# A graph-transformer layer on one core: the dense branch's attention, residual and normalization made per tile in the projections

## The chip, the cores and the metric

The kernel runs on one core of one Trainium2 chip. The metric is the device time of one execution in microseconds (us); the median of three runs is given. Besides the five engines TensorE (PE), VectorE (DVE), ScalarE (ACT), GpSimd (POOL) and SyncE (SP), the core has 16 DMA engines. A change of 0.3% can't be told from none.

## The reference, cut to what matters

6250 nodes of 256 numbers, 100000 edges sorted by target, four edge types, four heads of 64. `_layernorm` has no gain; all is float32.

```python
xn = layernorm(x)
# edge branch
xe = xn + segment_sum(edge_emb[type], src) / max(count, 1)
q, k, v = xe@Wq+bq, xe@Wk+bk, xe@Wv+bv
alpha = sum(q[dst]*k[src], per head) / 8
a = exp(alpha - segment_max(alpha, dst))
gnn = segment_sum(a*v[src], dst) / segment_sum(a, dst) + (xe@Ws + bs)
# dense branch: attention over features, so it is one matrix for all nodes
q, k, v = split(xn@w_qkv + b_qkv)
A = softmax(k.T @ v / 8)              # 64x64 for each head
x1 = xn + (q @ A.T)                   # = xn @ w_qf + b_qf
h = layernorm(x1)*norm_g + norm_b
mix = x1 + (gelu(h@w_fc1 + b_fc1) @ w_fc2 + b_fc2)     # 256 -> 768 -> 256
y = x + gnn + mix
out = y + experts(layernorm(y))       # 8 experts of three 256x256 layers, weighted by a softmax
```

## The kernel before

Nodes are worked in 49 tiles of 128 rows (`NW`). The stages follow each other on all engines; each engine's program is written out in order, and semaphores alone couple them. No scheduler decides anything.

**Preparation.** Sorting tables, the histogram of edge types (`r4x`), the normalized `x` in SBUF (`xnode`), also stored to DRAM as `xn_rows`, and the matrix `xn.T @ xn` for the dense attention.

**Projections.** Four tiles make a turn: `turn_types` transposes their type shares, `turn_x` transposes the nodes and adds the edge embeddings in PSUM (L1136, L1140), ACT (`upper`) and DVE (`lower`) split the result into a high and a low part. `project` (L1151) then makes q and skip in one product of 512 columns and k and v in another; each is six matmuls in a reduced float32 form (two halves of the contraction, three pairs of high and low parts). DVE (`evacuate`, L1609 to L1614) adds biases, keeps q in SBUF and adds `x` to skip; SP stores k and v (`kv_rows`) and `x` + skip (`sx_rows`). Between tiles `attend` makes, in eight small steps, the dense branch's matrix `w_qf` and bias `b_qf`.

**Edge pass.** 208 steps of four slots of 128 edges. POOL gathers k and v of the sources into a ring of 12 steps (four gathers a step, L811), after all of `kv_rows` and `sx_rows` is stored. In step i DVE makes one-hots (L1732), multiplies q and k (L1738), sums scores (L1744), weights v of step i-7 (L1791) and adds up the sums of step i-8 (L1805, or L1800 to L1803). PE spreads q to the edges of step i+2 (`spread_q`, L1275) and gathers up step i-7 (`gather_up`, L1286). Every fourth step the segment maxima of 16 slots go from DVE over PE and ACT (Exp) back (L1754 to L1786, L936).

The **dense branch** rides in the same steps: `dense` gives every eight steps a group g of two tiles and a phase p. PE: phase 0 the product with `w_qf` (L1231, full float32), phase 2 transposes, 3 to 5 the first large layer (L1246), 4 to 7 the second (L1253), 7 the next group's transposes (L1220). DVE: phase 0 bias, statistics and variance (L1701 to L1709), phase 1 normalization (L1712, L1714), phases 3 and 4 residual sums (L1718, L1720), phase 7 the last sum (L1726). ACT: Sqrt in phase 0, scaling in phase 2, Gelu in 3 to 5. The result goes to DRAM (`res_rows`).

**Experts.** 13 groups of three or four tiles, eight experts each. `first_part` prepares the next group between the experts of this one: in expert 0's place DVE divides the edge sums, adds `res_rows` (L1878) and takes statistics.

Of the kernel before, what the change touches and what calls it, by code (L numbers as in the profile page):

```python
# [24 lines left out]
def gps_layer_kernel(nc, x, src, dst, etype, edge_emb, Wq, bq, Wk, bk, Wv, bv, Ws, bs,  # L25
# [61 lines left out]
    def done(g):  # L87

        return g + (1 + CREDIT)
# [12 lines left out]
    xnD = nc.dram_tensor("xn_rows", [NW * P, D], F32, kind="Internal").ap()  # L102
# [15 lines left out]
    FC1 = {3: (0, 1), 4: (2, 3), 5: (4, 5)}  # L118
    FC2 = {4: (0,), 5: (1,), 6: (2, 3), 7: (4, 5)}

    with ExitStack() as ctx:
# [21 lines left out]
        m_st = sb("m_st", [P, TG * 6], F32)  # L143
        m_mv = sb("m_mv", [P, TG * 2], F32)
        m_rs = sb("m_rs", [P, TG], F32)
# [34 lines left out]
        emb = pre("emb", [3 * NTYPE, D], F32)  # L180
# [14 lines left out]
        part("gap8", [P, 9 * D + 2 * P + 512], F32)  # L195
        w_glow = part("w_glow", [P, 8 * D], F32R)
        part("gap9", [P, AN + 7400 - 17 * D - 2 * P - 512], F32)
        r4x = part("r4x", [P, 3 * NK], F32R)
        part("gap11", [P, 8 * NSP + NF * QW - 7400 - 3 * NK], F32)
        x_up = part("x_up", [P, 2 * NF * QW], F32R)  # L200
        x_low = part("x_low", [P, 2 * NF * QW], F32R)
        part("gap12", [P, RN + 3008 - 8 * NSP - 5 * NF * QW], F32)
        r4_T = part("r4_T", [3 * NTYPE, 2 * QW], F32R)
        part("gap13", [P, 4500 - 3008 - 2 * QW], F32)
        emb3 = part("emb3", [3 * NTYPE, D], F32R)
        part("gap10", [P, 7112 - 4500 - D], F32)
        w_gup = part("w_gup", [P, 8 * D], F32R)
        parts.close()

# [9 lines left out]
        m_x1 = mid("m_x1", [P, W4], F32)  # L219
# [31 lines left out]
        e_rest = sb("e_rest", [P, 1024], F32)  # L251
        f_res = sb("f_res", [P, WT], F32)
        f_split = sb("f_split", [P, 8 * WT], F32R)
# [3 lines left out]
        e_bol = sb("e_bol", [3 * NE, D + 4], F32)  # L257
        assert 2 * WE == 4 * D + AN and 4 * HG * SL + 2 * WE + 1024 + WT <= RING and 2 * WT <= HELD
# [96 lines left out]
        sxS = [work[:, 1560 + 256 * k:1560 + 256 * (k + 1)] for k in range(4)]  # L355
        zero_g = work[:, 2600:2600 + D + 1]
        r4T = [r4_T[:, QW * b:QW * (b + 1)] for b in range(2)]
        emb_low = work[0:3 * NTYPE, 4200:4200 + D]
        emb_at = [work[0:3 * NTYPE, 4200 + D + i:4200 + D + i + 1] for i in range(2)]
        ATT = {4 * r - 2: r for r in range(1, 9)}  # L360
        ATT_BD, ATT_EXP = 21, 5

        g_G = rows[:, 14 * NSP:14 * NSP + 2 * (D + 1)].rearrange("p (i e) -> p i e", i=2)
        g_U = rows[:, 13100:13100 + 2 * D].rearrange("p (i e) -> p i e", i=2)
        g_s = rows[0:1, 13700:13700 + D]
        g_t = rows[0:1, 13960:13960 + D]

# [18 lines left out]
        a_sm = cut(work, 0, 2 * C)  # L386
        a_bd = cut(work, 128, 2 * P)
        a_T = cut(work, 384, 2 * P)
        a_wT = cut(work, 640, 4 * P)
        a_bT = cut(work, 1152, 2 * P)  # L390
        a_row = cut(work, 1408, P)
        a_v = [cut(work, 1536 + 2 * i, 2) for i in range(4)]
# [38 lines left out]
        def _(sp):  # L431
# [58 lines left out]
            sp.wait_ge(sem("xn_made"), NW)  # L490
            sp.dma_start(xnD.rearrange("(t p) d -> p t d", p=P), nodes[:, X0:X0 + NW * D].rearrange("p (t d) -> p t d", d=D)).then_inc(sem("rows_out"), 16)
            for b in range(3):
                sp.dma_start(sxS[b], x[b * P:(b + 1) * P, :]).then_inc(sem(f"tile_moves{b}"), 16)
            sp.wait_ge(sem("rows_out"), 48)
            sp.wait_ge(sem("pen_out"), 16)

            def relq_load(i, c):
# [22 lines left out]
            def store(t):  # L520
# [4 lines left out]
                if t >= 1:  # L525
                    landed(t - 1)
# [1483 lines left out]
```

## Time and profile before

| | |
|---|---|
| Median of three runs | 2811.33 us (2808.03 to 2815.71) |
| The profiled execution | 2796.99 us, its span 2795.3 us |
| PE busy in the span | 2449.1 us (88%) |
| DVE busy | 2143.5 us (77%) |
| ACT busy | 1389.7 us (50%) |
| POOL busy | 923.9 us (33%) |

"Busy" is the time in which at least one instruction of the engine runs; PE's weight loads are counted apart (PEld). An idle time is put down to what ended last before it ("<-"); "issue" is a wait that the profile shows no cause of, "remote" one for an unknown queue. In the profile a full float32 matmul is recorded twice: eight records of L1231 are four matmuls. Numbers such as L1701 are lines of the kernel before; those of the kernel after are given as such.

### The profile page before, as it was taken

To read this page: it belongs to the slowest core of one execution; us is meant where nothing else is said; L and a number is where in the kernel's file an instruction comes from. 1 tells how busy PE (TensorE), PEld (TensorE's weight loads), DVE (VectorE), ACT (ScalarE), POOL (GpSimd) and SP (SyncE) were. 2 spreads that over 40 slices of the span, in tenths; PEclk is the share of its full clock that TensorE was granted. 3 is DMA by queue.
4 is the path that set the end of the run, shared out by engine and by line. 5 is a ranking of instruction groups with operands and counts; after the bars stand their busy time and mean duration, and the time that the engine had idled before them with its cause. 6 is when DMAs were issued, how large, how long until landed. Compare 5 with 4: busy or idle time off the path is not lost.

```text
span 2795.3 us, 42254 instructions
## 1 busy us (share of the span) xinstructions
PE 2449.1 (88%) x13352; PEld 2052.7 (73%) x13352; DVE 2143.5 (77%) x3905; ACT 1389.7 (50%) x2619; POOL 923.9 (33%) x891
## 2 busy tenths in 40 slices
PE   6478994799899889899888988867999999999998
PEld 4267773677677677777767777646988888888898
DVE  6797552898998989989898999857666666666665
ACT  5421110465566555656655656545555555555554
POOL 0140004566666666656656666600000000000000
PEclk9799997999999999999999999988999999999999
DMA  5131456566666666666666666630000000000000
GB/s 155 28 115 39 141 175 192 168 194 196 194 201 192 197 185 197 204 186 195 199 192 183 197 198 192 185 123 16 14 16 16 16 16 16 16 16 14 14 9 12
DMA packets 189689, 336.31 MB, mean 120 GB/s; under 512 B 31112, under 2 KB 128688, under 8 KB 189446
## 3 DMA queue, kind: packets, MB, share of 16 engines
q0 software_dynamic: 67104, 219.09, 26.1%
q1 hardware_dynamic: 122374, 114.53, 13.6%
q8 instruction: 117, 1.92, 0.3%
q14 instruction: 94, 0.77, 0.1%
HBM read 293.84 MB, written 40.48 MB: 120 GB/s over the span
## 4 chain that ended last, share of the span: by engine, by line
PE 70%; DVE 18%; issue 7%; another core or an unknown queue 2%; DVEq 1%; ACT 1%; DMA 0%; SPq 0%; POOL 0%; ACTq 0%; POOLq 0%
PE ps L1390 19%; PE ps L1286 11%; PE ps L1400 10%; PE ps L1275 8%; PE ps L1151 5%; PE ps L1253 3%; PE ps L1246 3%; DVE ring L1738 3%; DVE ring L1791 2%; DVE rows L1487 2%; PE ps L1064 2%; PE ps L1231 1%; DVE nodes L1805 1%; PE ps L1071 1%
## 5 line engine op out<-in xcount | busy, mean ns | idle before, releaser
L811 POOL DMA_INDIRECT ring<-kv_rows,idx x832 | 870.8, 1047 | 764.6 <-issue 261.8
L1390 PE MATMUL ps<-f_split,e_up 128*128 128x512 f32 (+1 forms) x1664 | 501.8, 383 | 7.2 <-DVE e_low L1952 6.8
L1275 PE MATMUL ps<-nodes,ohT 128*128 x1664 | 418.2, 396 | 96.8 <-issue 50.1
L1275 PEld LDWEIGHTS ps<-nodes,ohT 128*128 128x128 f32 x1664 | 321.0, 198 | 171.2 <-issue 124.4
L1286 PE MATMUL ps<-ring 128*128 128x260 f32 x1664 | 445.7, 414 | 0.0
L1928 DVE TENSOR_TENSOR f_split<-f_more,f_split 128x1024 fp32r<-128x1024 f32 (+1 forms) x208 | 242.0, 1164 | 237.0 <-ACT f_split L996 233.4
L990 ACT ACTIVATE f_more<-ps,e_rest 128x512 f32<-128x512 f32 (+1 forms) x416 | 289.1, 746 | 268.1 <-PE ps L1390 267.4
L1286 PEld LDWEIGHTS ps<-ring 128*128 128x128 f32 x1664 | 316.4, 200 | 43.4
L1390 PEld LDWEIGHTS ps<-f_split,e_up 128*128 128x128 f32 x1664 | 305.7, 190 | 55.4 <-DVE e_low L1952 7.5
L923 ACT ACTIVATE nodes<-ps 128x780 f32 x208 | 170.7, 820 | 296.0 <-PE ps L1286 265.1
L1390 PE MATMUL ps<-f_split,e_low 128*128 128x512 f32 (+1 forms) x832 | 315.3, 379 | 0.0
L1400 PE MATMUL ps<-e_up,f_split 128*128 128x256 f32 x1568 | 287.5, 284 | 4.0 <-DVE nodes L1944 4.0
L1738 DVE TENSOR_TENSOR ring<-ring,ps 128x1024 f32<-128x1024 f32 x208 | 252.3, 1213 | 41.5 <-remote 22.9
L1791 DVE TENSOR_TENSOR ring<-ring 128x1024 f32<-128x1024 f32 x208 | 253.1, 1217 | 17.5 <-ACT ring L936 12.9
L914 ACT ACTIVATE ring<-iota_f,relC 128x128 f32<-128x128 f32 x832 | 263.4, 392 | 0.0
L1400 PEld LDWEIGHTS ps<-e_up,f_split 128*128 128x128 f32 x1568 | 251.6, 192 | 11.2 <-issue 5.0
L1744 DVE TENSOR_REDUCE alpha<-ring 128x16 f32<-128x1024 f32 x208 | 254.0, 1221 | 7.1
L1400 PE MATMUL ps<-e_low,f_split 128*128 128x256 f32 x784 | 222.3, 284 | 0.0
L1390 PEld LDWEIGHTS ps<-f_split,e_low 128*128 128x128 f32 x832 | 157.6, 189 | 25.8
L996 ACT ACTIVATE f_split<-f_more 128x1024 fp32r<-128x1024 f32 (+1 forms) x104 | 105.1, 1011 | 128.7 <-PE ps L1390 128.7
L1944 DVE SCALAR_TENSOR_TENSOR nodes<-ps,small,nodes 128x256 f32<-128x256 f32 x392 | 162.6, 476 | 4.1 <-PE ps L1400 4.1
L1487 DVE TENSOR_TENSOR rows<-work,rows 128x1568 bf16<-128x1568 bf16 (+1 forms) x160 | 145.0, 954 | 24.2 <-PE ps L1064 23.3
(348 smaller groups left out, 3477.7 us busy)
## 6 DMA issues: line engine op xcount, KB each, us to landing
relq<-rel_rows SPq DMA_DIRECT2D x208, 128.0 KB
ring<-kv_rows,idx POOLq DMA_INDIRECT x832
kv_rows<-work SPq DMA_DIRECT2D x49, 256.0 KB, 2.2
xn_rows<-nodes SPq DMA_DIRECT2D x1, 6272.0 KB, 22.3
sx_rows<-work SPq DMA_DIRECT2D x49, 128.0 KB, 1.7
nodes<-in_x_dram SPq DMA_DIRECT2D x4, 1536.0 KB
work<-in_x_dram SPq DMA_DIRECT2D x48, 128.0 KB, 2.3
m_xn<-xn_rows SPq DMA_DIRECT2D x24, 256.0 KB
```

The source lines that it names most:

```text
L811: pool.indirect_dma_start(out=kvh(c)[:, g, 0:2 * D], out_offset=None, in_=kvD, in_offset=bass.IndirectOffsetOnAxis(ap=idx[c // KP][:, s:s ...
L914: ins = act.activation(kv[:, g, 0:P], iota_f[:, :], ACT.Abs, bias=relC[:, ds(j * HG + g, 1)], scale=-1.0)
L990: ins = act.activation(f_whole[l][:, m * QW:m * QW + n * P], bank(2 * l + m, 0, n * P), ACT.Relu, bias=e_sh[l][:, e * NF + m:e * NF + m + ...
L1275: last = pe.matmul(ps[:, 2048 + D * g:2048 + D * (g + 1)], ohT[c % 2][:, g * P:(g + 1) * P], nodes[:, ds(win[g] * AC + HG * AC, D)], start ...
L1286: last = pe.matmul(to, kvh(cj)[:, g, 0:P], kvh(cj)[:, g, D:SL], start=(g == 0), stop=False, skip_group_check=True)
L1390: last = pe.matmul(bank(2 * l + m, 0, n * P), e_parts[l][w][:, e, i, m * P:(m + 1) * P], src_[a][:, i * QW:i * QW + n * P], start=(i == 0 ...
L1400: last = pe.matmul(ps[:, 4 * 512 + t * D:4 * 512 + (t + 1) * D], f_h[1][a][:, i * QW + t * P:i * QW + (t + 1) * P], e_parts[2][w][:, e, i, ...
L1487: ins = dve.tensor_tensor(o[:, 0:G * n].rearrange("p (g m r) -> p g m r", g=G, r=2), twice(k[:, ds(c * 2 * G, 2 * G)]).unsqueeze(2).broadc ...
L1738: dve.tensor_tensor(k, k, ps[:, 2048:3072].rearrange("p (g d) -> p g d", g=HG), ALU.mult).then_inc(sem("prod_made"), 1)
L1744: dve.tensor_reduce(alpha[c // CH % 2][:, :].rearrange("p (h s) -> p s h", h=H)[:, c % CH * HG:(c % CH + 1) * HG, :], kvh(c)[:, :, 0:D].re ...
L1791: dve.tensor_tensor(v4, v4, kv[:, :, 2 * D:SL].unsqueeze(3).broadcast_to([P, HG, H, C]), ALU.mult).then_inc(sem("oh2_made"), 1)
L1928: dve.tensor_tensor(lo, whole, up.bitcast(F32), ALU.subtract).then_inc(sem(("h1_lo", "h2_lo")[l]), 1)
```

## The change

The dense branch's first half moves from the edge pass to the projections.

- `project` becomes a visit. Visits 0 to 11 make only q (256 columns) and k, v (512) of tiles 0 to 11; visits 12 to 48 also make skip and the attention product `x1` of the same tile in the same reduced form; visits 49 to 60 return to tiles 0 to 11 for skip and `x1` alone, from copies (`kept`) that ACT made of the first three turns. The products come after `w_qf` is ready; the skip weights become Ws + `w_qf`, so that `sx_rows` holds x + skip + x1 with all biases. Since the nodes then carry the edge embeddings, two rows are appended to the type shares that hold biases and take the embeddings' part out of `x1` (`c_mix`, made in a ninth step of `attend`).
- Per tile DVE takes statistics of `x1` in PSUM (`spreads`), ACT the root, DVE the scale and shift (`scales`), ACT the normalized rows (`normal`), and SP stores them (`z_rows`); `xn_rows` is gone.
- In the edge pass remain the transposes, the two large layers (first layer phases 0 to 2, second 3 to 5) and, in phase 6, ACT's copy of the result from PSUM; DVE has no dense work there.
- POOL's first three steps of gathers wait for `kv_rows` only; the fourth waits for the other stores.
- The experts' `first_part` loads `sx_rows` as well (`f_skip`) and adds it.

```diff
-    FC1 = {3: (0, 1), 4: (2, 3), 5: (4, 5)}
-    FC2 = {4: (0,), 5: (1,), 6: (2, 3), 7: (4, 5)}
+    FC1 = {0: (0, 1), 1: (2, 3), 2: (4, 5)}
+    FC2 = {3: (0, 1), 4: (2, 3), 5: (4, 5)}
+    EARLY = KEPT * QT
+    VISITS = NW + EARLY
...
+                if i == 3:
+                    for k in range(4):
+                        pool.wait_ge(sem(f"skip_moves{k}"), -(-(NW - k) // 4) * 32)
+                    for k in range(2):
+                        pool.wait_ge(sem(f"z_out{k}"), (NW - k + 1) // 2 * 16)
...
+            def root(n):
+                act.wait_ge(sem("z_var"), n + 1)
+                act.activation(z_rs[:, n % 2 * 2:n % 2 * 2 + 1], z_rs[:, n % 2 * 2:n % 2 * 2 + 1], ACT.Sqrt).then_inc(sem("z_std"), 1)
...
+            for v in range(EARLY, VISITS):
+                n = v - EARLY
+                if n >= 1:
+                    normal(n - 1)
+                if v in UPPER_AT:
+                    b = UPPER_AT[v]
+                    if b > KEPT + 1:
+                        turned(b)
+                    upper(b)
+                root(n)
...
-                if p == 0:
-                    act.wait_ge(sem("m_var"), g + 1)
-                    act.activation(m_rs[:, 0:n], m_rs[:, 0:n], ACT.Sqrt).then_inc(sem("m_std"), 1)
...
+                if p == 6:
+                    act.wait_ge(sem("fc2_ps"), g + 1)
...
+                    act.activation(m_sx[:, 0:n * D], bank(7, 0, n * D), ACT.Copy).then_inc(sem("m_out"), 1)
...
+                if v < NW:
+                    product(bank(6 + k), *cols(2 * D, 4 * D), None)
+                    if n > 0:
+                        pe.wait_ge(sem("qk_sb"), done(v - 1))
+                    product(q_ps(v), *cols(0, D), None).then_inc(sem("qk_ps"), 1)
+                if n >= 0:
+                    if n >= 2:
+                        pe.wait_ge(sem("z_made"), n - 1)
+                    product(SKIP[n % 2], *cols(D, 2 * D), c_mix[:, D:2 * D])
+                    product(X1[n % 2], wq_up, wq_low, c_mix[:, 0:D]).then_inc(sem("x1_ps"), 1)
...
+            for v in range(VISITS):
+                if v == EARLY:
+                    pe.wait_ge(sem("att_sb"), 10)
+                    pe.wait_ge(sem("skip_weights"), 2)
+                project(v)
...
+                if n >= 1:
+                    scales(n - 1)
...
-                g, p = dense(c, m)
-                if not known or 0 <= g < NG:
-                    mix(g, p, TG)
-                elif g == NG:
-                    mix(g, p, 1)
...
                     go(dve.tensor_tensor(y, y, rows_of(f_res), ALU.add))
+                    go(dve.tensor_tensor(y, y, rows_of(f_skip), ALU.add))
```

DVE in the projections, one tile of the middle. Before, with the bias of `attend` behind it; then after, one full visit and the next one's first rows:

```order
L1609 SCALAR_TENSOR_TENSOR nodes<-ps,b_gnn 128x256
L1612 TENSOR_TENSOR work<-ps,b_gnn 128x512
L1614 TENSOR_TENSOR work<-ps,work 128x256
L1661 COPY b_qf<-ps 128x256
L1609 SCALAR_TENSOR_TENSOR nodes<-ps,b_gnn 128x256
```

```order
L1721 SCALAR_TENSOR_TENSOR nodes<-ps,b_gnn 128x256
L1724 TENSOR_TENSOR work<-ps,b_gnn 128x512
L1740 RECIPROCAL z_rs<-z_rs 128x1
L1741 SCALAR_TENSOR_TENSOR z_rs<-z_mv,z_rs 128x1
L1731 TENSOR_TENSOR work<-ps,work 128x256
L1732 BN_STATS z_st<-ps 128x6
L1733 BN_AGGR z_mv<-z_st 128x2
L1734 TENSOR_SCALAR z_rs<-z_mv 128x1
L1721 SCALAR_TENSOR_TENSOR nodes<-ps,b_gnn 128x256
```

The scale of the tile before comes between this tile's q, k, v and its statistics; in the tail visits the first two rows are missing. DVE in the edge pass, from the product of one step with phase 0 to the next one-hot, before and after:

```order
L1738 TENSOR_TENSOR ring<-ring,ps 128x4x256
L1744 TENSOR_REDUCE alpha<-ring 128x4x4
L1791 TENSOR_TENSOR ring<-ring 128x4x256
L1794 TENSOR_LOAD row_box
L1794 ISA x2
L1805 ISA
L1805 SCALAR_TENSOR_TENSOR nodes<-nodes,follows,ps 128x260
L1786 TENSOR_SCALAR open_f<-ps,openC,keptC 128x4
L1701 TENSOR_TENSOR m_x<-ps,b_qf 128x512
L1703 BN_STATS m_st<-m_x 128x6 x2
L1705 MEMSET spare 128x1
L1707 BN_AGGR m_mv<-m_st 128x2 x2
```

```order
L1854 TENSOR_TENSOR ring<-ring,ps 128x4x256
L1860 TENSOR_REDUCE alpha<-ring 128x4x4
L1907 TENSOR_TENSOR ring<-ring 128x4x256
L1910 TENSOR_LOAD row_box
L1910 ISA x2
L1921 ISA
L1921 SCALAR_TENSOR_TENSOR nodes<-nodes,follows,ps 128x260
L1902 TENSOR_SCALAR open_f<-ps,openC,keptC 128x4
L1848 TENSOR_SCALAR ohT<-relq,iota_p 128x512
```

Behind `open_f` the next step's one-hot follows at once. PE at the start of the same step, before and after (`m_T` holds the transposed tiles, `alpha` the scores):

```order
L1275 MATMUL ps<-nodes,ohT 128x256
L1231 MATMUL ps<-w_qf,m_T 128x256 x4
L1267 TENSOR_LOAD row_box
L1263 TENSOR_LOAD row_box
L1311 MATMUL ps<-ident,alpha 64x128
L1281 MATMUL ps<-zeros 128x4 x3
```

```order
L1374 MATMUL ps<-nodes,ohT 128x256
L1344 MATMUL ps<-m_T,w_f 128x256 x4
L1366 TENSOR_LOAD row_box
L1362 TENSOR_LOAD row_box
L1410 MATMUL ps<-ident,alpha 64x128
L1380 MATMUL ps<-zeros 128x4 x3
```

The first large layer's matmuls stand where the attention product stood.

## Rows read from the trace of the kernel before

**Rows 1.** Windows by stage: busy us by engine (instructions), granted clock, DMA share, GB/s.

```profile
252.00:434.00 182.00, 177.16 (x812) 136.41 (x812) 90.55 (x201) 22.72 (x44) 0.00 (x0) 0.98 0.44 146
434.00:500.00 66.00, 24.67 (x81) 17.86 (x81) 22.74 (x41) 3.12 (x6) 40.37 (x43) 0.69 0.65 191
500.00:1845.00 1345.00, 1180.78 (x5975) 964.67 (x5975) 1202.33 (x2172) 786.00 (x1705) 830.41 (x790) 0.97 0.65 193
1930.00:2795.00 865.00, 854.30 (x5134) 771.63 (x5132) 572.36 (x1052) 442.61 (x615) 0.00 (x0) 1.00 0.05 15
```

**Rows 2.** Timeline of DVE, one dense group: start, us, instruction, [idle before, releaser].

```profile
1014.06 0.48 DVE L1732 TENSOR_SCALAR ohT<-relq,iota_p 128x512 f32<-128x512 bf16 x1
...
1021.37 0.69 DVE L1701 TENSOR_TENSOR m_x<-ps,b_qf 128x512 f32<-128x512 f32 x1 [2.73 <-PE ps L1231]
...
1023.25 0.49 DVE L1732 TENSOR_SCALAR ohT<-relq,iota_p 128x512 f32<-128x512 bf16 x1
...
1046.69 1.23 DVE L1791 TENSOR_TENSOR ring<-ring 128x1024 f32<-128x1024 f32 x1 [1.05 <-issue]
...
1065.07 0.15 DVE L1779 COPY carryC<-ps 64x2 f32<-64x2 f32 x1 [1.15 <-PE ps L1286]
...
1068.04 0.68 DVE L1726 TENSOR_TENSOR m_sx<-ps,m_sx 128x512 f32<-128x512 f32 x1
1068.64 0.47 DVE L1732 TENSOR_SCALAR ohT<-relq,iota_p 128x512 f32<-128x512 bf16 x1
```

**Rows 3.** Waits (total us, times, longest), and POOL's gathers, from 600 to 1800 us.

```profile
DVE carryC L1779 <- PE ps L1286: 26.4, 24, 1.5
DVE m_x L1701 <- PE ps L1231: 25.8, 20, 2.7
...
L811 POOL DMA_INDIRECT ring<-kv_rows,idx x719 | 755.2, 1050 | 446.9 <-PE ps L1286 222.4 <-issue 217.5 <-remote 7.0
```

**Rows 4.** Timelines of PE, POOL and DVE at the start of the edge pass.

```profile
434.56 1.99 PE L1275 MATMUL ps<-nodes,ohT 128*128 x8 [2.24 <-DVE ohT L1732]
...
446.51 3.75 PE L1275 MATMUL ps<-nodes,ohT 128*128 x8 [6.57 <-DVE ring L1738]
...
439.70 0.95 POOL L811 DMA_INDIRECT ring<-kv_rows,idx  x1 [0.30 <-issue]
...
475.00 1.22 DVE L1738 TENSOR_TENSOR ring<-ring,ps 128x1024 f32<-128x1024 f32 x1 [16.02 <-remote]
...
499.58 1.22 DVE L1738 TENSOR_TENSOR ring<-ring,ps 128x1024 f32<-128x1024 f32 x1
```

**Rows 5.** Timeline of DVE at the end of the edge pass, after the last dense tile.

```profile
1815.13 1.21 DVE L1738 TENSOR_TENSOR ring<-ring,ps 128x1024 f32<-128x1024 f32 x1
...
1819.17 1.23 DVE L1791 TENSOR_TENSOR ring<-ring 128x1024 f32<-128x1024 f32 x1 [1.57 <-ACT ring L936]
...
1838.57 1.21 DVE L1738 TENSOR_TENSOR ring<-ring,ps 128x1024 f32<-128x1024 f32 x1
```

**Rows 6.** Timeline of PE in the projections.

```profile
395.96 0.40 PE L1151 MATMUL ps<-w_gup,x_low 128*128 128x512 f32 x1
396.20 0.40 PE L1151 MATMUL ps<-w_gup,x_up 128*128 128x512 f32 x1
...
407.14 1.03 PE L1136 MATMUL ps<-ident,nodes 128*128 128x128 f32 x8
...
408.77 0.51 PE L1151 MATMUL ps<-w_gup,x_up 128*128 128x512 f32 x1
```

**Rows 7.** Timelines of DVE and PE in the experts, one group.

```profile
2135.57 1.22 DVE L1878 TENSOR_TENSOR nodes<-nodes,f_res 128x1024 f32<-128x1024 f32 x1
...
2141.77 1.65 DVE L1944 SCALAR_TENSOR_TENSOR nodes<-ps,small,nodes 128x256 f32<-128x256 f32 x4
...
2143.92 0.40 PE L1400 MATMUL ps<-e_up,f_split 128*128 128x256 f32 x2
...
2144.28 0.40 PE L1400 MATMUL ps<-e_up,f_split 128*128 128x256 f32 x2
```

**Rows 8.** Groups of instructions on DVE, 600 to 1800 us: busy us, mean ns.

```profile
L1703 DVE BATCH_NORM_STATS2 m_st<-m_x 128x6 f32<-128x256 f32 x43 | 16.2, 419 | 0.7
```

**Rows 9.** The chain of work that ended last, two pieces: start, us.

```profile
1049.38 1.86 PE ps L1286 x8
1051.24 1.75 PE ps L1275 x8
```

More of the change, by code:

```diff
@@ L384, in cut @@
             return t[:, at:at + n]
[L386 to L392, printed above, removed]
+        a_sm = cut(rows, 0, 2 * C)
+        a_bd = cut(rows, 128, 2 * P)
+        a_T = cut(rows, 384, 2 * P)
+        a_wT = cut(rows, 640, 4 * P)
+        a_bT = cut(rows, 1152, 2 * P)
+        a_row = cut(work, 1112, P)
+        a_v = [cut(rows, 1408 + 2 * i, 2) for i in range(4)]
         e_w = [e_raw01[:, 0:WE], e_raw01[:, WE:2 * WE], e_raw2[:, :]]
@@ L866, in upper @@
             def upper(b):
-                n = min(QT, NW - b * QT) * P
-                act.wait_ge(sem("xE_ps"), b + 1)
+                n = min(QT, NW - b * QT) * P if b < NQ else QW
+                if b < NQ:
+                    act.wait_ge(sem("xE_ps"), b + 1)
+                if b < KEPT:
+                    for i in range(NF):
+                        last = act.activation(kept[:, (b * NF + i) * QW:(b * NF + i) * QW + n], bank(i, 0, n), ACT.Copy)
+                    last.then_inc(sem("kept_sb"), 1)
@@ L870, in upper @@
                 if b >= 2:
-                    act.wait_ge(sem("qk_ps"), done(b * QT - QT - 1))
+                    act.wait_ge(sem("qk_ps"), done(min(LAST_OF[b - 2], NW - 1)))
+                    if LAST_OF[b - 2] >= EARLY:
+                        act.wait_ge(sem("x1_ps"), LAST_OF[b - 2] - EARLY + 1)
                 for i in range(NF):
-                    last = act.activation(xU[b % 2][:, i * QW:i * QW + n], bank(i, 0, n), ACT.Copy)
+                    at = (b - NQ) * NF + i
+                    whole = bank(i, 0, n) if b < NQ else kept[:, at * QW:(at + 1) * QW]
@@ new lines, in _ @@
+            for i in range(2):
+                act.activation(a_sm[:, i * C:(i + 1) * C], a_sm[:, i * C:(i + 1) * C], ACT.Exp, bias=a_v[1][:, i:i + 1],
+                               scale=1.0 / C ** 0.5, accum_out=a_v[2][:, i:i + 1]).then_inc(sem("a_exp"), 1)
+            upper(2)
+            turned(3)
+            act.wait_ge(sem("skip_weights"), 1)
+            act.activation(w_up[:, :, D:2 * D], w_gnn[:, :, D:2 * D], ACT.Copy)
+            act.activation(wq_up, w_qf, ACT.Copy).then_inc(sem("w_upper"), 1)
@@ L1193, in attend @@
                         last = pe.matmul(at(i * P, P), a_bT[:, i * P:(i + 1) * P], a_T[:, i * P:(i + 1) * P], start=True, stop=True)
+                if r == 9:
+                    for h in range(2):
+                        for i in range(2):
+                            pe.matmul(at(h * D, D)[0:NR, :], embT[:, i * NR:(i + 1) * NR], w_qf[:, i, :], start=(i == 0), stop=False)
+                        last = pe.matmul(at(h * D, D)[0:NR, :], last_two, c_bias[:, h * D:(h + 1) * D], start=False, stop=True)
                 last.then_inc(sem("att_ps"), 1)
```

477 lines of the change are left out of this document (260 added, 217 removed).

## The prediction

> **What bounds the kernel now.** I read first the table of windows [rows 1], which splits the span of 2795.3 us into stages: preparation up to 252 us, the projections from 252 to 434, a start of the edge pass that is nearly idle (434 to 500), the steady edge pass to 1845, a drain, and the experts from 1930 on. The edge pass is almost half the span, and in it DVE is busy 1202 of 1345 us and PE 1181: two engines near their limit, coupled step by step. The projections are bound by PE alone (177 of 182 us), the experts too (854 of 865 us).
>
> The second view is DVE's timeline over one group of eight edge steps [rows 2]; the dense branch handles two tiles in each such group. From one one-hot (L1732) to that eight steps later pass 54.58 us. Dense work on DVE is 1.88 us between L1701 and the next L1732, and 0.82, 0.72, 0.71 and 0.60 us in later steps of the group, 4.73 in all. Stalls are 2.73 us ahead of L1701 (DVE waits for the attention product, which PE makes only after the step's spread of q), 1.05, 0.22 and 1.15 us: 5.15. So DVE's own edge work is 54.58 - 4.73 - 5.15 = 44.7 us, or 5.59 a step.
>
> The third view, the list of waits from 600 to 1800 us [rows 3], says how typical that is: 25.8 us of DVE's waits stand before the dense product and 26.4 us before the carries. One step there is 1200/180 = 6.67 us (180 of the 208 steps have their product in it), and from the seventh product at 499.58 [rows 4] to the last at 1838.57 [rows 5] the 201 steps take 6.66 us each.
>
> **The change part by part.**
>
> *Projections, PE.* One matmul of 512 columns starts 0.233 us after the one before it (395.96 to 396.20), and a turn of four tiles costs 1.63 us (407.14 to 408.77) [rows 6] and some 0.4 more for the types. One of 256 columns takes 0.12 us: three of them in 0.36, from 2143.92 to 2144.28 [rows 7]. Before, a tile is 12 x 0.233 = 2.8 us. Now keys and values are 6 x 0.233 = 1.40, q, skip and attention 18 x 0.12 = 2.16, and the two added type rows 0.24: 3.80. With a quarter of a turn (0.5) that is 4.3 us for each of the 37 visits that do both jobs: 159, and I add 2 for a wait of each turn on ACT's copy of the types, which now stands behind ACT's normalization. The first twelve visits make only q, k and v: 12 x 2.12 = 25.4, three turns 6, the attention matrices 12 (what is left of the 182 us after 49 x 2.8, 13 turns of about 2 and the 7.5 us of start and end), a new ninth step of them 2.3, and at visit 12 one stall of about 2.4 in which DVE finishes visit 11 and makes two low halves: 48. The twelve tail visits cost PE only 14 x 0.12 = 1.68 each, and there a chain is longer: DVE adds, takes statistics, aggregates and adds epsilon (0.41, 0.42, 0.16 and 0.17, as the dense branch's statistics [rows 8] and the small steps behind L1701 do now), ACT's root takes 0.20, DVE's two scalings 0.3, gaps 0.3, that is 1.95; with two buffers every second visit also sees PE's 1.68, so I take 2.15 a visit, 26, plus 5 for the first low half and its successors. Total 48 + 161 + 31, plus 7.3 at the start (the kept copies put one pair of ACT copies, 1.1, into the chain ahead of the first product) and 2.4 at the end for the last normalization: 250 against 182. With four or five more tiny DVE steps before it (1 us) this is **+69**, with bounds of 55 and 85.
>
> DVE has in a full visit 0.94 (q, k, v), 1.2 (statistics), 0.4 (scalings) and 0.3 (low half): 2.9 us beside PE's 4.3, so it is covered; if that cover were gone, PE would pay the difference. SP issues four DMAs a visit instead of three, at about 0.4 each, 1.6 beside 4.3. PE's new wait, ahead of skip, is for the tile normalized two visits earlier; behind it stand both products and the next tile's k and v, and in full visits it is covered by 2.1 us of k, v and q and the products before. SP waits for each tile's variance before its stores; behind that are the next loads of x, three tiles ahead (12 us), so DVE doesn't see it.
>
> Once more on the tail: in [rows 4] the same eight matmuls of L1275 take 1.99 us at 434.56 and 3.75 at 446.51, after 6.57 us idle; the mean granted clock of that stage is 0.69 [rows 1], so part of it ran at 1.2 GHz. The Trainium skill ("TensorE: Matmul & The Clock Gate", Part 1) says that an idle TensorE falls back to the lower clock, which this trace shows; by it the tail could cost 12 x 1.68 = 20 us more, if PE's gaps of half a microsecond were to count as idle. I don't take it.
>
> *Start of the edge pass.* POOL's first gathers go out from 437 us on, after everything was stored, one each 1.25 us (0.95 and a gap of 0.30); DVE's fourth product (L1738) comes at 475.00 and the seventh at 499.58 [rows 4]. Now the first three steps' gathers (12 x 1.25 us) need only the key and value rows, ready after visit 48, and run under the tail. From the fourth on they wait as all did before. So the chain starts with 15 us less: **-15**, bounds 0 (if the fourth product's 475.00 hangs on something else, such as code or tables) and -25.
>
> *Edge pass.* It loses 4.73 us of DVE work per group and the 2.73 us stall; on PE the attention product (1.73) and four transposes (0.44); on ACT two of its four table loads, 1.28 us each, while a copy of 0.6 us takes the place of another; ACT, busy 786 of 1345 us, is no bound. PE keeps the large layers, now 1.73 us in each of six steps of a group. By the chain's rows [rows 9] its gather-up takes 1.86 us and its spread 1.75; with the zeroing (0.1) a step is 3.7 us, eight are 29.7, the large layers 10.4, four transposes 0.44 and the small products 2.4: 42.9, or 5.37 a step, under DVE's 5.59. POOL needs 4 x (1.05 + 0.30) = 5.40 [rows 3]. So the floor is DVE's 5.59. What is late next is the chain at every fourth step, from DVE's differences over ACT's Exp, PE's transposes and gather-up and ACT's copy to DVE's weighting. The steps at the end with no dense work at all show what remains: four steps from 1815.13 to 1838.57 [rows 5], 5.86 each, with one stall of 1.57 us (at 1819.17) for that chain. I take 5.80, between the floor and that: (6.66 - 5.80) x 201 = **-173**. Bounds: 5.59 gives -215, 6.2 (all the present stalls but the one at L1701 stay and PE adds some) -92.
>
> *Experts.* DVE gets one more 1024-wide addition per group of tiles, 1.22 us like L1878, and SP one more load, a group ahead. The cover is thin: the accumulation at 2141.77 takes 1.65 us and ends at 2143.42, and PE's next last layer, which overwrites its PSUM, starts at 2143.92 [rows 7]. Half a microsecond of slack against 1.26: 0.76 late in each of 12 groups, and 1.2 exposed in the first: **+10**, bounds 1 and 15.
>
> Sum: 69 - 15 - 173 + 10 = -109. The profiled execution took 2796.99 us, 14 less than the median of 2811.33; by its own time it would be 2688, and on the median, which I forecast, 2702.
>
> **The rivals.**
>
> *The coupling stays.* PE in the first four steps of a group has 22.8 us of work against DVE's 22.2, so it comes late to the fourth, and each wait before the carries remains (26.4 us in [rows 3] speak for it; that they stood behind PE's two heaviest steps, 2.6 us of dense work, which are gone, speaks against). At 6.2 a step the gain is 92: 2783.
>
> *DVE runs at its floor.* 5.6 a step and a start shorter by 25: 2811 + 69 - 25 - 213 + 10 = 2652.
>
> *The normalization is not covered.* If PE waited in each of the 37 full visits for the round DVE, ACT, DVE, ACT, some 2.6 us with the 0.6 of the scaling copy, it would cost 96: 2798. Two buffers and 3.8 us of PE work between speak against it.
>
> *The gathers pace the edge pass (the slower side).* If POOL and its transfers are what limits, the step stays at 6.66, nothing is gained there and the rest is paid: 2811 + 69 - 15 + 10 = 2875. It decides at 6.34 a step, where the gain of 64 just covers the costs; POOL's start-to-start would have to go from 1.35 to 1.59 us. Against it: POOL now waits 222 us for PE in 1200, and the DMA engines are at 0.65 [rows 1, 3]. For it: one gather takes 0.95 us when DVE is idle [rows 4], 1.05 in the pass [rows 3]. The Trainium skill ("SBUF — State Buffer", Who interferes with whom) says that GpSimd cannot write descriptors while DVE runs certain copies and tensor_scalar forms; the trace agrees in direction (0.95 and 1.05), and the change removes two such DVE operations a group but packs the others closer.
>
> That the work isn't moved at all is excluded: the order of DVE's instructions no longer has it in the edge pass.
>
> **How the numbers follow.** Forecast 0.60 (2702, own range 2655 to 2750); coupling 0.20 (2783); floor 0.11 (2652); normalization 0.03 (2798); gathers 0.06 (2875). The range of 2640 to 2785 holds the first three but for their tails. Changes of 0.3% (8 us) can't be told from none; under 2803 lie the first and the third, nine tenths of the coupling and half of the normalization: 0.90; within 0.3%: 0.04; slower: 0.06.
>
> **What would show it.** After: projections from about 252 to 502 with PE over 90% busy up to visit 48 and about 75% in the tail; the first gathers some 30 us before the end of the tail; DVE's product every 5.8 us, with few waits over 1 us but that before its weighting; POOL's wait for PE falling from 1.2 to 0.4 us a step; PE waits of under 1 us on the accumulation in the experts. The forecast is wrong if DVE's own busy time per step is 5.6 and the step still over 6.2, or if PE is under 85% busy in the full visits.

## The result

The changed kernel takes 2893.36 us (median of 4, 2889.96 to 2901.42), the kernel before in the same job 2810.07 (2808.03 to 2815.71). The ratio is 1.0302, with a 95% interval of 1.0275 to 1.0330: slower by 3%, where 2702 was forecast. The profiled execution has a span of 2899.7 us, that of before 2795.3: 104 us to account for.

Windows of the changed kernel by stage (columns as in [rows 1]): full visits, tail of the projections, steady edge pass, experts.

```profile
309.00:494.00 185.00, 184.78 (x1082) 150.34 (x1083) 95.60 (x311) 41.50 (x101) 0.00 (x0) 1.00 0.40 138
494.00:548.00 54.00, 46.58 (x176) 36.24 (x173) 21.86 (x85) 13.40 (x34) 11.88 (x12) 0.62 0.45 141
...
1000.00:1900.00 900.00, 777.22 (x3857) 636.74 (x3858) 741.56 (x1255) 484.60 (x1101) 595.28 (x544) 0.95 0.65 190
...
1975.00:2880.00 905.00, 875.48 (x5189) 785.49 (x5190) 611.09 (x1108) 465.65 (x640) 0.00 (x0) 0.98 0.06 21
```

DVE's timeline, its seventh and its last product (L1854, which was L1738 in [rows 4, 5]):

```profile
595.47 1.22 DVE L1854 TENSOR_TENSOR ring<-ring,ps 128x1024 f32<-128x1024 f32 x1
...
1927.56 1.21 DVE L1854 TENSOR_TENSOR ring<-ring,ps 128x1024 f32<-128x1024 f32 x1
```

POOL's timeline, its first gather:

```profile
495.18 1.08 POOL L852 DMA_INDIRECT ring<-kv_rows,idx  x1 [306.78 <-DMA kv_rows<-work]
```

The seventh product comes at 595.5 instead of 499.6, the last one 1332.1 us later instead of 1339.0 (6.63 us a step, before 6.66), and from there to the end are 972.2 us instead of 956.7: +96, -7, +15. So the projections cost more than forecast and the edge pass gave nothing, although DVE is busy only 742 of 900 us in it (82%; [rows 1] have 89%) and PE 86%. The waits had to tell why. The page's chain of work that ended last:

```profile
PE 57%; DVE 25%; issue 9%; another core or an unknown queue 5%; ACT 2%; DVEq 1%; DMA 0%; ACTq 0%; SPq 0%
```

Groups of instructions from 600 to 1800 us (busy us, mean ns | idle before, by releaser), of the changed kernel:

```profile
L1854 DVE TENSOR_TENSOR ring<-ring,ps 128x1024 f32<-128x1024 f32 x181 | 219.4, 1212 | 68.8 <-remote 61.5 <-PE ps L1374 5.4 <-issue 0.4
L1003 ACT ACTIVATE nodes<-ps 128x780 f32 x180 | 147.8, 821 | 258.8 <-PE ps L1385 140.7 <-remote 83.1 <-issue 34.0
```

and of the kernel before:

```profile
L1738 DVE TENSOR_TENSOR ring<-ring,ps 128x1024 f32<-128x1024 f32 x180 | 218.3, 1213 | 5.6 <-remote 3.7 <-PE ps L1275 0.5
L923 ACT ACTIVATE nodes<-ps 128x780 f32 x180 | 147.7, 820 | 249.3 <-PE ps L1286 226.8 <-issue 15.6 <-remote 5.7
```

"Remote" is a wait whose end the profile can lay to no instruction. DVE had none to speak of before its product, and now 61.5 us; ACT had 5.7 and now 83.1 before it copies the sums. One such place, timeline of all engines:

```profile
1023.06 1.89 PE L1374 MATMUL ps<-nodes,ohT 128*128 x8
...
1027.65 2.00 PE L1385 MATMUL ps<-ring 128*128 128x260 f32 x8
...
1029.01 0.95 POOL L852 DMA_INDIRECT ring<-kv_rows,idx  x1 [0.30 <-issue]
1031.24 1.22 DVE L1854 TENSOR_TENSOR ring<-ring,ps 128x1024 f32<-128x1024 f32 x1 [3.91 <-remote]
1031.49 0.23 ACT L1016 ACTIVATE ring<-ps 128x64 f32<-128x64 f32 x1 [3.14 <-remote]
1032.15 0.82 ACT L1003 ACTIVATE nodes<-ps 128x780 f32 x1 [0.44 <-issue]
1032.18 0.95 POOL L852 DMA_INDIRECT ring<-kv_rows,idx  x1 [2.22 <-remote]
```

PE's spread of q ends at 1024.95 and its gather-up at 1029.65. DVE waits for the first, ACT and POOL for the second, and all three stand still until 1031.2 to 1032.2. The trace also records when each semaphore is raised: the one that follows the spread stands at 1031.15, 6.2 us after the last matmul, the next three of PE, that of the gather-up among them, at 1031.26, 1031.29 and 1031.41. So PE's signals are late, in a bunch. I call late what is recorded over 0.3 us after the modelled end of its matmul, and count a bunch as one place: 199 places in the steady edge pass of this trace, 116 in that of before (what counts as one bunch moves both by some 10%), none in the experts or the full visits. DVE's four most frequent instructions have theirs within 0.02 us in nine of ten cases. Two cautions: the ends of matmuls are modelled, so that late matmuls aren't excluded, though the starts of the matmuls behind (1024.79, 1027.65) follow each other as usual; and records are missing in this trace, of DVE's signals too (its one-hot has 151 of 208), so that a wait can also be "remote" because the record that ended it is missing. That is a behaviour, not yet a cause.

### The profile page after: what moved, and what is told of

Its sections match the earlier page's. It is cut to its first block, busy times and chain, and to the rows that moved or that the text cites. A ratio compares the mean times of both kernels' runs of the same rounds, so it can differ in the third digit from the quotient of the medians.

```text
span 2899.7 us, 43174 instructions
## 1 busy us (share of the span) xinstructions
PE 2529.0 (87%) x13770; PEld 2115.4 (73%) x13770; DVE 2112.5 (73%) x3864; ACT 1365.3 (47%) x2661; POOL 957.9 (33%) x891
## 4 chain that ended last, share of the span: by engine, by line
PE 57%; DVE 25%; issue 9%; another core or an unknown queue 5%; ACT 2%; DVEq 1%; DMA 0%; ACTq 0%; SPq 0%
PE ps L1489 15%; PE ps L1499 9%; PE ps L1385 8%; PE ps L1239 7%; PE ps L1374 5%; DVE ring L1854 4%; DVE ring L1907 2%; PE ps L1344 2%; DVE rows L1587 2%; DVE nodes L1921 2%; PE ps L1144 1%; DVE nodes L2056 1%; PE ps L1242 1%; DVE ohT L1848 1%
## 5 line engine op out<-in xcount | busy, mean ns | idle before, releaser
L852 POOL DMA_INDIRECT ring<-kv_rows,idx x832 | 904.7, 1087 | 821.7 <-DMA kv_rows<-work 306.8
L1374 PE MATMUL ps<-nodes,ohT 128*128 x1664 | 433.5, 407 | 72.5 <-DVE ring L1854 53.6
L1385 PE MATMUL ps<-ring 128*128 128x260 f32 x1664 | 455.5, 421 | 0.0
L1374 PEld LDWEIGHTS ps<-nodes,ohT 128*128 128x128 f32 x1664 | 338.4, 206 | 140.4 <-issue 83.9
L1854 DVE TENSOR_TENSOR ring<-ring,ps 128x1024 f32<-128x1024 f32 x208 | 252.2, 1212 | 104.9 <-remote 88.1
```

The costliest lines, as they stand in the source:

```text
L852: pool.indirect_dma_start(out=kvh(c)[:, g, 0:2 * D], out_offset=None, in_=kvD, in_offset=bass.IndirectOffsetOnAxis(ap=idx[c // KP][:, s:s ...
L1374: last = pe.matmul(ps[:, 2048 + D * g:2048 + D * (g + 1)], ohT[c % 2][:, g * P:(g + 1) * P], nodes[:, ds(win[g] * AC + HG * AC, D)], start ...
L1385: last = pe.matmul(to, kvh(cj)[:, g, 0:P], kvh(cj)[:, g, D:SL], start=(g == 0), stop=False, skip_group_check=True)
L1854: dve.tensor_tensor(k, k, ps[:, 2048:3072].rearrange("p (g d) -> p g d", g=HG), ALU.mult).then_inc(sem("prod_made"), 1)
```

## The experiments

Two questions: what the late signals depend on, and why the projections cost so much more. The eighteen runs came in five jobs, each with the kernel before on the same chip; the job matters, as will be seen. "Step" is the time from the seventh to the last product over 201. Medians, and for single executions their time, in us:

| job, chip | late signals | kernel before | changed kernel | others |
|---|---|---|---|---|
| result | yes | 2810 (step 6.66) | 2893 (6.63) | |
| 1, chip 11 | none | 2734 (one execution) | | no_layers 2731 (5.96), half_rows 2716 (5.83), half_gathers 2711 (5.86), no_type_rows 2661 (5.83) |
| 2, chip 13 | yes | 2805 (6.68) | 2899 (6.60) | padded_types 2871 (6.64) |
| 3, chip 0 | none | 2729 (6.45) | 2709 (5.84) | no_layers 2729 (5.94), half_gathers 2712 (5.86) |
| 4, chip 12 | none | 2729 | | padded_filled 2678 (5.83), half_gathers 2713 (5.85), half_rows 2707 (5.84), no_layers 2734 (5.96) |
| 5, chip 11 | yes | 2809 | | padded_types 2873 (6.65), half_gathers 2748 (5.86), no_layers 2923 (6.71) |

### First job: load, bytes, gathers, type rows

no_layers:

```diff
@@ PE, mix @@
+                if p == 6 and nxt:
+                    mix_turn(g + 1, nxt)
+                return
@@ ACT, mix, p == 6, and no Gelu @@
-                    act.activation(m_sx[:, 0:n * D], bank(7, 0, n * D), ACT.Copy).then_inc(sem("m_out"), 1)
+                    act.activation(m_sx[:, 0:n * D], m_T[:, 0:n * D], ACT.Copy).then_inc(sem("m_out"), 1)
```

> The changed kernel without the two large layers and the Gelu in the edge pass (left out: PE's twelve matmuls and ACT's six Gelus of a group; what is stored is the turned tile instead). The turn of the next tiles, loads and stores stay. In the changed kernel DVE's product comes every 6.63 us (595.47 to 1927.56, 201 steps). If PE's load and the queue behind it set that step, it loses 1.3 us of PE work a step and falls to 5.6 to 5.9, the whole to some 2740. If the gathers and their transfers pace the pass, it stays within 6.5 to 6.7 and the whole within 15 us of 2893. If only the order of PE's signals behind the layers matters, something between, near 6.2.

half_rows and half_gathers (the count that a wait for a buffer's gathers looks for follows):

```diff
+                wide, rows_in = (2 * D, kvD) if i < KP else (D, kvD.rearrange("r (h d) -> (r h) d", h=2))
-                    pool.indirect_dma_start(out=kvh(c)[:, g, 0:2 * D], out_offset=None, in_=kvD,
+                    pool.indirect_dma_start(out=kvh(c)[:, g, 0:wide], out_offset=None, in_=rows_in,
...
-                for g in range(HG):
+                for g in range(HG if i < KP else HG // 2):
```

> The changed kernel with gathers that move half a row (256 instead of 512 values) from the 13th step on; the number of gathers and everything else stay (left out: the value half, and the rows are others). If the bytes moved, or memory traffic that holds up signals, pace the edge pass, the step falls from 6.63 to 6.1 or less; if it is the issue on POOL or PE and DVE, it stays within 0.1 of 6.63.

> The changed kernel with two gathers a step instead of four from the 13th step on (left out: half of the windows' rows). Bytes as in half_rows, and POOL's work halved too. If POOL's issue is what paces (4 x 1.39 us = 5.6, plus waits for PE), the step falls below that of half_rows; if only bytes matter, both give the same; if PE and DVE alone set the step, it stays at 6.6 in both.

no_type_rows:

```diff
-                    product(SKIP[n % 2], *cols(D, 2 * D), c_mix[:, D:2 * D])
-                    product(X1[n % 2], wq_up, wq_low, c_mix[:, 0:D])...
+                    product(SKIP[n % 2], *cols(D, 2 * D), None)
+                    product(X1[n % 2], wq_up, wq_low, None)...
```

> The changed kernel without the two matmuls over 14 rows (L1242) at the end of the skip and of the attention product of each tile (left out: the types' part of these products). A start-to-start reading of the trace gives 0.52 us for each of them in place of the 0.12 in my sum: 0.213 before and 0.307 behind it. If that is so, a full visit falls from 5.0 to 4.0 us (37 visits: 38 us less) and a tail visit, at half clock, by up to 1 us, so the projections take some 245 to 255 us instead of 297. If the 14 rows cost 0.12 each, the stage changes by under 12 us.

All four came out at 5.83 to 5.96 a step, no_type_rows too, which leaves the edge pass as it is, and the kernel before took 2734 in this job. No trace of the job has a late signal. For the edge pass the job decided nothing but this: something other than the work differs between jobs. For the projections it did: POOL's first gather, which comes when the full visits are through, stands at 456.7, against 495.2 in the result's trace and 491.1 in the changed kernel of job 3 below. A full visit takes 4.1 us without the type rows and 5.0 with them.

### Second and third job: the pair again, and padded type rows

> The changed kernel, unchanged. In the first four runs nothing of the kind was seen that fills the two traces shown: signals of PE that arrive 0.3 to 6 us after the matmul that sends them (in 199 places of the changed kernel's edge pass, 116 of the kernel's before), and the kernel before took 2734 us there instead of 2810. Theory A: the loss lies in those late signals, which belong to the executions and not to the work: without them the edge pass takes 5.8 a step as no_type_rows did, the whole 2700 (no_type_rows' 2661 and some 40 for the type rows), faster than the kernel before by about 1.2%. Theory B: the change itself makes them, and they come back here: 2890 or so against before's 2734 to 2810.

> The kernel before, for its trace beside after_again. If its time is 2734 and no signals are late, its step should be (2810 - 2734) / 201 = 0.38 below the 6.66 of the trace shown, 6.3; with late signals 6.6. In either case the projections take 182 us.

padded_types:

```diff
-        c_mix = part_at("c_mix", WORK0 + 2648, [NR, 2 * D], F32R)
-        r4_T = part_at("r4_T", WORK0 + 3160, [NR, 2 * QW], F32R)
+        c_mix = part_at("c_mix", WORK0 + 2648, [P, 2 * D], F32R)
+        r4_T = part_at("r4_T", WORK0 + 3160, [P, 2 * QW], F32R)
+            link(dve.memset(r4_T[:, :].bitcast(F32), 0.0))
+                    dve.memset(c_mix[:, :].bitcast(F32), 0.0)
```

(the copies into these tiles, and the types' product of L1224, keep to their first NR rows)

> The changed kernel with the two type matmuls of each tile over 128 rows instead of 14: rows 14 to 127 of both operands are zeros, set once. Nothing is left out. If what costs 0.52 us is the change from 128 rows to 14 and back, each takes some 0.12 like its neighbours, a full visit 4.3 us and a tail visit about 1 us less, and the whole comes out 35 to 45 us below after_again, with 12 us or so of it in the tail. If the cost lies in the matmul itself, nothing is gained.

Theory B seemed to hold: in job 2 the late signals were back (195 places in the changed kernel, 132 in the one before), with a ratio of 1.0329 (1.0297 to 1.0361). So the pair ran once more.

> The changed kernel, unchanged, once more. after_again had 195 places of late signals (2899), as the trace shown; the kernels of the first job, on another chip (11, after_again was on 13), had none. Theory C: whether PE's signals come late belongs to the chip. On a chip without them the changed kernel takes 2700 (no_type_rows 2661 plus the 30 that padding took off, plus what is left of the type rows) and beats the kernel before (2734 there) by 1%; on a chip with them 2890 to 2900 against 2805 to 2810. A time between, or late signals in one of the kernels alone, speaks against C.

> The kernel before, for its trace. By theory C without late signals 2734, with a step of 6.3 and none late; on a chip with them 2807 and 6.67, some 120 places late.

> no_layers again (left out: the two large layers and Gelu of the edge pass). Where no signals are late it took 2731 and 5.96 a step. On a chip with late signals: if they come from PE being kept busy behind waiting instructions, there are few here and the step stays under 6.1; if from the gathers' traffic, as many as in after_again (some 195) and the step is 6.2 or more.

> half_gathers again (left out: two of four gathers of a step from the 13th on). Without late signals 2711 and 5.86 a step. On a chip with late signals: if the gathers' traffic makes them, their number falls by half or more and the step to 6.2 or less; if it has nothing to do with the gathers, 180 to 200 places and 6.6 a step.

In job 3 no signal is late and the same two kernels stand at 0.9919 (0.9903 to 0.9936): the change is faster by 0.8%. The windows from 600 to 1700 us of the changed kernel, of the kernel before, and of the changed kernel in the trace of the result:

```profile
600.00:1700.00 1100.00, 1040.96 (x5360) 864.44 (x5359) 1020.28 (x1740) 676.58 (x1530) 835.31 (x759) 0.97 0.74 217
```

```profile
600.00:1700.00 1100.00, 995.95 (x5078) 818.19 (x5077) 1015.04 (x1837) 666.27 (x1438) 707.25 (x678) 0.98 0.67 199
```

```profile
600.00:1700.00 1100.00, 951.59 (x4708) 778.74 (x4707) 905.61 (x1531) 594.75 (x1349) 721.41 (x659) 0.95 0.65 189
```

DVE is busy 93% of the time there, 82% in the result's trace, and "remote" is gone from the waits before its product (600 to 1800 us, job 3):

```profile
L1854 DVE TENSOR_TENSOR ring<-ring,ps 128x1024 f32<-128x1024 f32 x196 | 237.0, 1209 | 3.0 <-PE ps L1374 1.3
L1003 ACT ACTIVATE nodes<-ps 128x780 f32 x205 | 168.4, 821 | 178.3 <-PE ps L1385 152.5 <-issue 23.7
```

Padding took 28.5 us off (2899 to 2871), where 35 to 45 were expected: POOL's first gather stands 25 us earlier and the seventh product 40 us, but the 201 steps took 9 us more (6.60 and 6.64 a step). The full visits fell from 5.0 to 4.3 us. A timeline of PE shows the same piece of a visit, first in the changed kernel, then in padded_again:

```profile
331.81 0.28 PE L1239 MATMUL ps<-w_gup,x_low 128*128 128x256 f32 x1
332.02 0.38 PE L1242 MATMUL ps<-c_mix,r_T 14*128 14x256 f32 x1
332.33 0.38 PE L1239 MATMUL ps<-wq_up,x_up 128*128 128x256 f32 x1
332.55 0.28 PE L1239 MATMUL ps<-wq_low,x_up 128*128 128x256 f32 x1
```

```profile
333.30 0.28 PE L1239 MATMUL ps<-w_gup,x_low 128*128 128x256 f32 x1
333.42 0.28 PE L1242 MATMUL ps<-c_mix,r_T 128*128 128x256 f32 x1
333.53 0.28 PE L1239 MATMUL ps<-wq_up,x_up 128*128 128x256 f32 x1
```

With 14 rows 0.52 us pass from the matmul ahead of it to the one behind, with 128 rows 0.23; and the one behind has its own successor 0.22 later instead of 0.12. That makes 0.39 us for a switch to 14 rows and back, on top of the matmul's own 0.12. The Trainium skill ("TensorE: Matmul & The Clock Gate", Why this matters for your kernels) says that a matmul over 32 rows takes as long as one over 128. No row here shows one by itself; among neighbours of 128 rows the trace differs, and the measurement decides.

### Fourth and fifth job: what the late signals depend on

padded_filled is padded_types with

```diff
+                    if NW <= v < VISITS - 1:
+                        product(bank(3, 0, D), *cols(0, D), None)
```

> padded_types, and in the first eleven of the twelve visits at the end of the projections, in which PE waits, six more matmuls of 256 columns into an unused bank (q's product once more, read by nobody). PE's clock was at 1.2 GHz in most of that stretch. If keeping PE busy holds it at 2.4, a visit costs 2.2 to 3 us instead of 3.5 and 5 to 15 us are gained on padded_types (which was 28.5 us below after_again on chip 13); if the chain over DVE and ACT sets the visit, nothing is gained or up to 8 us lost. On a chip without late signals: 2665 to 2685 against the 2709 of after_third.

> half_gathers again (left out: two of four gathers of a step from the 13th on). Where no signals are late it takes 2711 and 5.86 a step. On a chip with late signals: if the number of gathers and of their landing signals makes them, they fall to half or less of 195 and the step to 6.2 or less; if neither gathers nor bytes matter, 180 to 200 and 6.6.

> half_rows again (left out: the value half of each row from the 13th step on; as many gathers and signals as before). Without late signals 2716 and 5.83 a step. On a chip with late signals: if bytes make them, they fall as in half_gathers; if the number of gathers and signals does, they stay at some 195 and the step at 6.6.

> no_layers again (left out: the two large layers and Gelu of the edge pass). Without late signals 2730 and 5.95 a step. On a chip with late signals: if PE's load behind waiting instructions matters, few are late and the step stays under 6.1; if only traffic matters, as many as in after_again, and the step is 6.2 or more.

Job 4 was again one without late signals. padded_filled took 2678 there, 0.9812 of the kernel before (0.9795 to 0.9828): it beats that one, and the 2709 that the changed kernel took in job 3, whose kernel before took the same 2729. Windows of the tail, the changed kernel in job 3 and padded_filled:

```profile
491.00:543.00 52.00, 47.05 (x172) 36.86 (x172) 21.07 (x81) 12.29 (x31) 11.62 (x12) 0.57 0.47 147
```

```profile
466.00:503.00 37.00, 31.75 (x238) 31.12 (x238) 20.44 (x79) 11.88 (x31) 11.69 (x12) 0.91 0.65 203
```

The tail fell from 52 to 37 us and its clock rose from 0.57 to 0.91. That doesn't show that the filler held the clock, because the unchanged tail moves by as much. The variants no_layers, half_rows and half_gathers change only the edge pass; with the changed kernel's own, thirteen traces have the same tail. From the statistics of visit 48 to those of visit 60 it took 39.2 to 54.2 us, with a clock of 0.83 down to 0.58. Windows inside the tail, of the result's trace and of no_layers (job 1):

```profile
516.00:543.00 27.00, 27.00 (x92) 21.24 (x91) 9.74 (x38) 6.68 (x16) 0.00 (x0) 0.50 0.31 100
```

```profile
506.00:530.00 24.00, 22.21 (x127) 17.13 (x126) 14.59 (x58) 8.36 (x21) 0.68 (x1) 1.00 0.54 175
```

A visit is 14 matmuls, so it took 4.1 us (27 x 14 / 92) at 1.2 GHz and 2.6 at 2.4, with the same instructions. Padding alone (padded_types and padded_again, both in jobs with late signals) gave 42 us at 0.84, padded_filled 37.5 at 0.91. What part padding and filler have in the tail stays open.

> padded_types again. Without late signals: if the filler matmuls of padded_filled (2678) gained nothing, it takes the same 2675 to 2680, if they gained what the clock lost, 2680 to 2690. With late signals: 2865 to 2875 as on chip 13, 1.023 times the kernel before.

> half_gathers again (left out: two of four gathers of a step from the 13th on). Without late signals 2711 to 2713 and 5.86 a step. On a chip with late signals: if the gathers and their landing signals make them, half of 195 or fewer and a step under 6.2; if not, 180 to 200 and 6.6.

> no_layers again (left out: the two large layers and Gelu of the edge pass). Without late signals 2730 to 2733 and 5.95 a step. On a chip with late signals: if PE's load behind waiting instructions matters, few are late and the step stays under 6.1; if only traffic matters, as many as in after_again and 6.2 or more.

Job 5 had late signals, on chip 11, where job 1 had none: theory C falls. Each job has them in all of its traces (with half the gathers in five places) or in none, and they don't go by the chip's number. And here the cases part. The window from 600 to 1700 us of no_layers_fourth, and ACT's wait before its copy of the sums there (total us, times, longest; 600 to 1800 us):

```profile
600.00:1700.00 1100.00, 816.01 (x3663) 642.85 (x3664) 890.07 (x1505) 481.50 (x1160) 718.37 (x648) 0.85 0.65 186
```

```profile
ACT nodes L1012 <- remote: 135.2, 38, 5.9
```

The same of half_gathers_fourth, the second as the group of ACT's copies:

```profile
600.00:1700.00 1100.00, 1042.71 (x5343) 863.72 (x5343) 1020.24 (x1731) 670.38 (x1518) 434.25 (x374) 0.97 0.46 126
```

```profile
L1003 ACT ACTIVATE nodes<-ps 128x780 f32 x203 | 166.5, 820 | 182.5 <-PE ps L1385 156.8 <-issue 23.3
```

Without PE's large layers there are still 115 late places, and the step is 6.71. With half the gathers there are 5, and the step is 5.86 as in the jobs without. Its whole is 37 us above the 2711 of job 1, and 35 of them stand before the seventh product (at 594.6 against 559.6): 4 up to visit 48, 8 in the tail, whose clock was lower (0.68 against 0.83), and 22 between the tail and that product, among the twelve steps whose gathers were left whole. So in such a job the full set of gathers holds the edge pass at 6.6 to 6.7 us a step, whatever the engines have to do: 6.66 and 6.68 in the kernel before, 6.63 and 6.60 in the changed one, 6.64 and 6.65 padded, 6.71 without layers. That half the gathers free it rests on one execution.

Slower transfers are not it: a DMA packet of 4096 bytes takes 220 ns on average in the steady pass of the result's trace and 215 in job 3's. Nor is it POOL's issuing by itself, since job 3 has the same gathers at 5.84 a step. Whether the number of gathers does it or their bytes is open: half_rows met no such job. Counted from the trace's records of signals, 188 steps of the steady pass have 19,198 from transfers in the changed kernel and 19,894 in the one before (job 3), 102 and 106 a step, and 65 with half the gathers. At 6.6 to 6.7 us a step that is 15.2 to 15.9 per us in the jobs with late signals, for four kernels with different work; in job 3 it is 16.4 and 17.5. A ceiling near 16 per us fits, and so would one on bytes. One more sign points at the signals' way: with late signals the trace holds only 8,227 to 8,922 of these records, under half, and 10,954 of some 12,200 with half the gathers. Whether recording has a part in the lateness can't be told, and this rival stands; the timed executions of a job agree with its profiled one to within 0.7%.

## Why the prediction was wrong

| from, to | forecast | result | job 3 |
|---|---|---|---|
| seventh product later | 69 - 15 = +54 | +96 | +99 |
| 201 steps | -173 | -7 | -123 |
| last product to end | +10 | +15 | +8 |
| sum | -109 | +104 | -16 |

*The edge pass* is the step that failed. Where no signal is late its size came out right, 5.84 a step against the 5.80 forecast, but not its floor: I had put DVE at 5.59 a step and PE at 5.37, and in job 3 PE is busy 1041 of 1100 us and DVE 1020, 5.53 and 5.42 a step. So the hit on 5.80 is luck in part. Two things more were wrong. The base: of the 6.66 us I laid all above 5.59 to dense work and coupling, but without late signals the kernel before takes 6.45, so 0.21 x 201 = 42 us of the forecast gain were not there to be had; with 0.04 x 201 for the size that makes -123 of the -173. And in a job with late signals almost none of the rest is paid out (-7), because the gathers hold the pass; the sign named for being wrong, DVE busy for 5.6 us of a step and the step over 6.2, came: 5.5 and 6.63. That was the rival "the gathers pace the edge pass", with 0.06 and 2875 us, against 2893. Its outcome came true and its condition didn't: I had tied it to POOL's start-to-start at 1.59 us. POOL's gathers in the changed kernel:

```profile
L852 POOL DMA_INDIRECT ring<-kv_rows,idx x720 | 788.6, 1095 | 413.4 <-issue 231.1 <-PE ps L1385 102.9 <-remote 79.4
```

A gather takes 1.10 us and a gap of 0.30, 1.40 and not 1.59, and POOL still idles. What was slow was not the issue but the signals afterwards, and I had argued against the rival from POOL's waits and the DMA engines' share alone. A hint stood in the trace of before, unread. From its list of waits, 600 to 1800 us (total us, times, longest):

```profile
ACT m_gT L906 <- remote: 35.0, 9, 6.0
ACT m_T L891 <- remote: 9.2, 2, 4.6
```

These are waits of ACT for PE, of 4 to 6 us, with no releaser. They stood under the dense branch's lines, and so I would have counted them as part of what was to be moved. In job 3 the same list has no "remote" wait for either kernel.

*The projections* were mis-sized: 296 us (251.3 to 547.6) where 250 were forecast. The early visits took 57.6 with the start, for 55.3. The full visits, from 308.9 to 495.2, took 5.0 us each instead of 4.3; the failed term is "the two added type rows 0.24", two matmuls priced like their neighbours of 128 rows: by the timeline above they cost about 1.0. padded_again, where they cost what I had taken, gives the forecast 4.3 (312.0 to 471.9). The tail took 52 us instead of the 33 of its visits and the last normalization. Matmuls of 256 columns start there 0.21 us apart, not 0.12: PE ran at 1.2 GHz, with a mean granted clock of 0.62. It had two gaps over 0.3 us, of 2.3 and 3.1, and was busy 46.6 of 54 us. Both terms were too small: at 2.4 GHz a tail visit takes 2.6 us (no_layers, above) where 2.15 were forecast, which is the type rows again, and at 1.2 GHz 4.1. I had set the lower clock's 20 us aside, and the tail cost 19 more; that these agree is luck, since part of the 19 is the type rows and the same tail took 39 to 54 us. The Trainium skill ("TensorE: Matmul & The Clock Gate", Part 1), which I cited, has an idle TensorE fall back to the lower clock. The trace agrees in that the clock fell within the first gap (at 495.3; PE idle from 494.4 to 496.6) and 0.7 us behind the second (at 515.7). Then it stayed at 1.2 GHz through 27 us in which PE was busy throughout.

*Start and experts* held. From the end of the projections to the seventh product there are 48 us instead of 66, -18 for the -15 forecast. This stage is slower too where signals are late: from POOL's first gather to the seventh product the kernel before takes 63 us in the result's trace and 41 in job 3. From the last product on the kernel takes 15 us more in the result and 8 in job 3, for +10. The normalization was covered in the full visits, where PE is busy 184.8 of 185 us. In the experts the page's group of PE's last layer shows the thin cover (idle before it; 4.0 us in the kernel before):

```profile
L1499 PE MATMUL ps<-e_up,f_split 128*128 128x256 f32 x1568 | 288.4, 284 | 8.8 <-DVE nodes L2056 8.8
```

That is 4.8 us more where I had priced 12 x 0.76 = 9.1. But the experts as a whole, from their first matmul to the end, take 907.6 us instead of 894.3, and 907.4 instead of 896.3 in job 3: 11 to 13 more, so the price was right in sum and only partly in its place. The rest of the 15 and the 8 lies between the last product and the experts (+2 and -3).

The change itself is worth -0.8% in one sort of job and +3% in another. The range of 2640 to 2785 would have held the first (2709) only, and by luck: there the kernel before was itself some 80 us faster than the one I forecast from, and the change gained 20 us, not 109.

## What to carry over

Before a stage is priced by how full its engines are, sum the waits whose releaser the profile can't name. A few of 4 to 6 us each, on several engines at once, are a reason to ask whether transfers and their signals hold the stage; where they did here, work taken off the engines bought nothing and fewer gathers did. Price a matmul by the time between its neighbours, with the same rows ahead and behind; a short one among full ones can be made full with zeros. And price a new stretch in which PE has to wait now and then at both of its clocks: the same tail took 39 to 54 us.

## What the runs showed of the hardware

Signals of PE were recorded up to 6.5 us after the modelled end of the matmul that raises them (result's trace, steady edge pass), in bunches, in all traces of one job and in none of another, even on a chip of the same number. The kernel before moves by 3.0% between such jobs, the changed kernel by 7%, and the order of the two turns round: one job is not enough for a change of this size.

Less work on PE made the edge pass slower where nothing was late: 5.94 to 5.96 a step in no_layers against 5.84. Its window in job 1:

```profile
600.00:1700.00 1100.00, 878.63 (x4147) 697.25 (x4147) 999.44 (x1704) 544.88 (x1312) 806.82 (x743) 0.89 0.73 212
```

The mean granted clock is 0.89 there against 0.97; of these 1100 us PE had 1.2 GHz in 225 to 237 in the three jobs without late signals, instead of 58. That the clock alone makes the difference isn't shown.

The granted clock isn't fixed by the instructions: thirteen traces of the same tail have means from 0.58 to 0.83 and take 54 to 39 us, and in one of them PE was busy for 27 us on end at 1.2 GHz.
